# A graph layer on one core: wa for the edge weighing in two PSUM banks, TensorE's phases over three pairs of banks, and a new order of VectorE's work

## The chip, the cores and the metric

The kernel runs on one core of one Trainium2 chip. The metric is the time of one execution in microseconds (us) on the device. A core has TensorE (matmuls), VectorE, ScalarE, GpSimd and SyncE (SP); the first four compute, and SP, ScalarE and GpSimd issue DMAs here. In the rows they are PE (PEld its weight loads), DVE, ACT, POOL and SP.

## The reference

```
h = relu(layernorm(x))                                   # x 512 x 1024
feat = concat(h[src], h[dst])                            # 8704 edges
e_hh, e_oo, e_ho = relu(feat[...] @ W + b)               # 256, 1280 and 7168 edges, W 2048 x 1024 each
logit = e_f @ W_a + b_a
alpha = softmax of logit over the edges with the same dst
z = segment_sum(alpha * h[src], dst)
new = relu(concat(h, z) @ W_n + b_n)                     # W_hn for nodes 0..127, W_on for the others
out = x + new
```

All of it is float32. setup_inputs makes the edges sorted by dst.

## The kernel before, in words

**Edges of two kinds.** For the HO and OO edges, feat @ W is P[src] + Q[dst], with P and Q the products of the 512 nodes with the upper and the lower half of W (P with the bias). TensorE makes P and Q, they are stored in DRAM, and GpSimd gathers their rows for tiles of 128 edges: 56 HO tiles and 10 OO tiles. For each tile VectorE adds the two gathered rows in two halves (line 635), and weighs: relu, times wa, and a sum over 1024 columns, in one instruction (line 638), whose result is the edges' logit. GpSimd scatters the logits into tables in DRAM with a cell for each pair of nodes. The 256 HH edges (two tiles) go through a full product of their features (line 1038), half of the columns at a time, and VectorE weighs each half in its bank (line 719, weigh_hh).

**Weights.** All weights come in 40 chunks of 1 MB through four places (raw); SP issues the load of chunk c once TensorE has used chunk c - 4 (load, line 272). ScalarE and VectorE split a chunk in an upper part w_hi (line 343) and the rest w_lo (line 576), and a product is three matmuls: upper by upper, upper by rest, rest by upper (lines 909 to 911). A chunk is 4 slices (k) by 4 blocks of nodes (b) by 3 matmuls, 48 in all.

**TensorE's order**, which is written out: node_products phases 0, 1, 2 and right_products (chunks 0 to 7, HO; the halves of P, then of Q), then four phases for OO (chunks 8 to 15), among them transposes of the HH rows; then the HH edges, two halves of 16 slices, each slice followed by a group of the counting (count_group, line 1014), which counts the edges of each pair of nodes as a product of one-hot rows (VectorE, line 672) and step rows (ScalarE, line 423); then the products of h with the node weights (TOP), those that z will need (G), and the tail, where the attention is made from the tables.

**Banks.** PSUM has eight banks. Before, an even phase wrote banks 0 to 3 and an odd one banks 4 to 7, and a phase's banks were emptied while the next phase ran: by VectorE for HO's P (evacuate_p, line 620; VectorE adds the bias), by ScalarE for the others. evacuate_p(0) writes stage[:, 0], which is also the source of five DMAs that clear the pair tables, so it waits for these (s_tabs).

**VectorE's order** is a list written by hand of tiles, splits, one-hot groups and unpackings of counts. Its one-hot group g waits for TensorE's group g - 16. peak_hh (line 748) takes the maximum of the HH pair table, which SP loads behind the load of chunk 35, and that waits for TensorE's use of chunk 31. Behind peak_hh come the last tiles, g_lo (the rest part of G's products, line 741), peak_ho, and the tail.

## Time and profile before

| | us |
|---|---|
| three runs | 452.58, 463.50, 467.38 (median 463.50) |
| profiled execution | 460.47 |
| its span on the core | 458.6 |
| TensorE busy in the span | 428.7 (93%) |
| VectorE | 327.0 (71%) |
| ScalarE | 146.5 (32%) |
| GpSimd | 247.4 (54%) |

The span is from the first to the last instruction in the trace, the profiled execution's own time is 1.9 us more. Busy time is an average over stages with different limits, so it is read by stretches. A row of the timeline has the start, the duration, the engine, the line of the kernel, what is written and read, how many instructions stand behind each other, and in brackets how long the engine was idle before it and what ended that.

### The profile page before, as it was taken

To read this page: it belongs to the slowest core of one execution; us is meant where nothing else is said; L and a number is where in the kernel's file an instruction comes from. 1 tells how busy PE (TensorE), PEld (TensorE's weight loads), DVE (VectorE), ACT (ScalarE), POOL (GpSimd) and SP (SyncE) were. 2 spreads that over 40 slices of the span, in tenths; PEclk is the share of its full clock that TensorE was granted. 3 is DMA by queue.
4 is the path that set the end of the run, shared out by engine and by line. 5 is a ranking of instruction groups with operands and counts; after the bars stand their busy time and mean duration, and the time that the engine had idled before them with its cause. 6 is when DMAs were issued, how large, how long until landed. Compare 5 with 4: busy or idle time off the path is not lost.

```text
span 458.6 us, 4884 instructions
## 1 busy us (share of the span) xinstructions
PE 428.7 (93%) x1698; PEld 301.1 (66%) x1698; DVE 327.0 (71%) x614; ACT 146.5 (32%) x216; POOL 247.4 (54%) x215
## 2 busy tenths in 40 slices
PE   0999999889999999999778999999999999798996
PEld 0788888678888888864223444467778888564844
DVE  5782362023699998697735999986999289999723
ACT  3841121044131333556234850121333120603200
POOL 3030006600688887777775787877888668710000
PEclk9999999999999999999999999999999999999999
DMA  8989857995945476958657766687788998369111
GB/s 329 370 332 395 351 213 264 414 400 189 345 152 172 136 258 190 323 180 289 198 146 236 265 199 216 214 302 280 265 278 303 403 363 324 95 189 361 47 69 69
DMA packets 40456, 116.02 MB, mean 253 GB/s; under 512 B 13625, under 2 KB 13625, under 8 KB 34672
## 3 DMA queue, kind: packets, MB, share of 16 engines
q1 hardware_dynamic: 14400, 64.07, 37.4%
q0 software_dynamic: 21760, 43.26, 28.7%
q10 hardware_dynamic: 4272, 8.39, 4.8%
q8 instruction: 13, 0.21, 0.2%
q14 instruction: 11, 0.09, 0.1%
HBM read 125.93 MB, written 17.86 MB: 314 GB/s over the span
## 4 chain that ended last, share of the span: by engine, by line
PE 75%; DVE 7%; DMA 6%; issue 4%; another core or an unknown queue 3%; ACT 2%; POOL 1%; SPq 0%; POOLq 0%; DVEq 0%
PE bank L911 15%; PE bank L910 15%; PE bank L909 15%; PE bank L1038 10%; PE bank L1014 6%; DMA stage<-pairs_hh 4%; PE bank L1128 3%; PE bank L1063 3%; DVE gath L635 2%; ACT step_rows L423 2%; PE bank L1103 2%; PE bank L1117 1%; PE bank L1119 1%; PE bank L1118 1%
## 5 line engine op out<-in xcount | busy, mean ns | idle before, releaser
L909 PE MATMUL bank<-w_hi,h_t 128*128 128x512 f32 x368 | 144.6, 393 | 0.2 <-issue 0.2
L911 PE MATMUL bank<-w_hi,h_t 128*128 128x512 f32 x368 | 143.4, 390 | 1.3 <-issue 1.3
L910 PE MATMUL bank<-g_raw,h_t 128*128 128x512 f32 x368 | 143.4, 390 | 1.0 <-issue 1.0
L1202 POOL DMA_INDIRECT gath<-q_ho,q_index x56 | 70.4, 1256 | 39.9 <-DMA q_ho<-stage 23.0
L576 DVE TENSOR_TENSOR g_raw<-raw,w_hi 128x512 fp32r<-128x512 f32 x96 | 60.0, 686 | 43.5 <-ACT w_hi L343 43.4
L343 ACT ACTIVATE w_hi<-raw 128x1024 fp32r<-128x1024 f32 x48 | 48.3, 1060 | 112.3 <-PE bank L911 35.2
L635 DVE TENSOR_TENSOR gath<-gath 128x512 f32<-128x512 f32 x110 | 70.9, 685 | 17.4 <-DMA gath<-q_ho,q_index 10.7
L911 PEld LDWEIGHTS bank<-w_hi,h_t 128*128 128x128 f32 x368 | 69.2, 188 | 16.8 <-issue 2.6
L910 PEld LDWEIGHTS bank<-g_raw,h_t 128*128 128x128 f32 x368 | 69.2, 188 | 15.8 <-issue 1.6
L909 PEld LDWEIGHTS bank<-w_hi,h_t 128*128 128x128 f32 x368 | 69.3, 188 | 15.1 <-issue 0.7
L1195 POOL DMA_INDIRECT gath<-p_ho,i_src x45 | 50.6, 1125 | 50.6 <-DMA p_ho<-stage 37.2
L638 DVE SCALAR_TENSOR_TENSOR gath<-gath,wa 128x1024 f32<-128x1024 f32 x55 | 67.4, 1225 | 1.9
L1038 PE MATMUL bank<-raw,feat 128*128 128x512 f32 x128 | 63.2, 595 | 5.8 <-issue 4.6
L423 ACT ACTIVATE step_rows<-node_row,step_at 128x512 bf16<-128x512 f16 x68 | 43.8, 713 | 31.4 <-remote 22.1
L1038 PEld LDWEIGHTS bank<-raw,feat 128*128 128x128 f32 x128 | 24.0, 189 | 29.5 <-issue 25.5
L1214 POOL DMA_INDIRECT pairs_ho<-logit,cell x28 | 34.7, 1239 | 14.5 <-issue 7.0
L1214 POOL DMA_INDIRECT pairs_ho_odd<-logit,cell x28 | 33.5, 1195 | 9.9 <-issue 7.3
L1014 PE MATMUL bank<-step_rows,count_rows 128*128 128x512 bf16 x136 | 35.7, 379 | 1.4 <-issue 1.1
L1014 PEld LDWEIGHTS bank<-step_rows,count_rows 128*128 128x128 bf16 x136 | 13.0, 98 | 29.7 <-issue 21.3
L672 DVE TENSOR_SCALAR count_rows<-node_row,dst_at 128x256 bf16<-128x256 f16 x68 | 19.4, 360 | 14.5 <-remote 14.5
L1088 PE MATMUL bank<-pick 128*128 128x512 f32 x70 | 18.1, 405 | 3.3 <-DVE gath L638 3.0
L1088 PEld LDWEIGHTS bank<-pick 128*128 128x128 f32 x70 | 12.4, 188 | 8.9 <-DVE gath L638 3.1
(159 smaller groups left out, 377.5 us busy)
## 6 DMA issues: line engine op xcount, KB each, us to landing
raw<-w_chunks SPq DMA_DIRECT2D x40, 1024.0 KB
gath<-x SPq DMA_DIRECT2D x4, 512.0 KB, 5.0
h_dram<-h_sb SPq DMA_DIRECT2D x1, 2048.0 KB, 11.6
p_ho<-stage ACTq DMA_DIRECT2D x2, 1024.0 KB
p_oo<-stage ACTq DMA_DIRECT2D x2, 1024.0 KB
q_oo<-stage ACTq DMA_DIRECT2D x2, 1024.0 KB
x_place<-x SPq DMA_DIRECT2D x2, 1024.0 KB, 8.8
out<-partial SPq DMA_DIRECT2D x8, 256.0 KB, 2.0
```

Of the source, the lines that this page charges most:

```text
L423: i = nc.scalar.activation(row_src(g)[:, j], node_row[:, :], ACT.Sign, bias=step_at[:, t:t + 1])
L576: i = nc.vector.tensor_tensor(w_lo[:, c % RAW, k], raw[:, c % RAW, k], w_hi[:, upper(c), k].bitcast(f32), ALU.subtract)
L635: i = nc.vector.tensor_tensor(p[:, cols], p[:, cols], q[:, cols], ALU.add)
L638: nc.vector.scalar_tensor_tensor(out=p, in0=p, scalar=0.0, in1=wa[:, :], op0=ALU.max, op1=ALU.mult, accum_out=logit[:, at:at + 1]).then_in ...
L909: nc.tensor.matmul(to, hi, w_high, start=first, stop=False)
L910: nc.tensor.matmul(to, hi, w_low, start=False, stop=False)
L911: return nc.tensor.matmul(to, lo, w_high, start=False, stop=last)
L1014: i = nc.tensor.matmul(bank[PART_BANKS[part] + b][:, :], row_dst[:, g % HOTS, j, b * P:(b + 1) * P], row_src(g)[:, j], start=(g, j) == (fi ...
L1038: m = nc.tensor.matmul(bank[4 * half + e][:, :], feat[:, kk, e * P:(e + 1) * P], raw[:, c % RAW, k], start=False, stop=kk == 2 * KT - 1)
L1195: nc.gpsimd.indirect_dma_start(edge_p[:, slot], None, node_tab[kind][0][:, :], bass.IndirectOffsetOnAxis(ap=i_src[:, at:at + 1], axis=0)). ...
L1202: nc.gpsimd.indirect_dma_start(edge_q[:, slot], None, node_tab[kind][1][:, :], bass.IndirectOffsetOnAxis(ap=q_index[:, at:at + 1], axis=0) ...
L1214: nc.gpsimd.indirect_dma_start(pair_tab[kind][:, :], bass.IndirectOffsetOnAxis(ap=cell[:, at:at + 1], axis=0), logit[:, at:at + 1], None). ...
```

## The change

Two of the eight banks (6 and 7, now wa_places) hold wa, copied there once by ScalarE (copy_wa), and the weighing of the tiles reads wa from them. The six other banks are three pairs. A phase uses two pairs; the next one begins with the third pair, and its second pair is the one that the phase before it used first. So a chunk's matmuls run over k for blocks 0 and 1, and then over k for blocks 2 and 3, and before the second pair's first matmul stands a wait (second_pair). HH, counting, TOP and G get other banks and other waits. VectorE's order is another one.

```diff
-PART_BANKS = (2, 6, 2, 6)
+PART_BANKS = (4, 0, 2, 0)
+HH_BANKS = (2, 4)
+TOP_PAIRS = ((1, 0), (2, 1))
+G_PAIRS = ((0, 2), (1, 0))
...
+        def phase_bank(phase, b):
+            return bank[2 * ((2 * phase + b // 2) % 3) + b % 2]
...
+            def copy_wa():
+                act.wait_ge(s_const, 32)
+                act.wait_ge(s_tlo, KT)
+                for half in range(NHALF):
+                    i = nc.scalar.activation(wa_places[:, half], wa[:, half * HALF:(half + 1) * HALF], ACT.Copy)
+                i.then_inc(s_wa, 1)
...
-                nc.vector.scalar_tensor_tensor(out=p, in0=p, scalar=0.0, in1=wa[:, :], op0=ALU.max, op1=ALU.mult,
+                nc.vector.scalar_tensor_tensor(out=p, in0=p, scalar=0.0, in1=wa_places.rearrange("p a d -> p (a d)"), op0=ALU.max, op1=ALU.mult,
                                                accum_out=logit[:, at:at + 1]).then_inc(s_logit, 1)
...
+            def second_pair(phase):
+                if phase in (1, 2):
+                    pe.wait_ge(s_pev, phase + 1)
+                if phase == 4:
+                    pe.wait_ge(s_qev, Q_EVACS[1] + 2)
+                if phase in (5, 6):
+                    pe.wait_ge(s_pev, phase - 1)
+                if phase == 7:
+                    pe.wait_ge(s_qev, Q_EVACS[3])
...
             node_products(PH_HO, 1)
-            pe.wait_ge(s_pev, 2)
             node_products(PH_HO, 2)
-            pe.wait_ge(s_pev, 3)
             right_products()
...
-                if g == first and part == 1:
+                if g == first and part == 0:
                     pe.wait_ge(s_qev, Q_EVACS[4])
-                if g == first and part >= 2:
-                    pe.wait_ge(s_cev, part - 1)
+                if g == first and part == 2:
+                    pe.wait_ge(s_hhhalf, 1)
+                if g == first and part == 3:
+                    pe.wait_ge(s_cev, 2)
...
             for half in range(NHALF):
+                if half:
+                    pe.wait_ge(s_cev, 1)
                 for j in range(4):
                     c = PH_HH + 4 * half + j
...
+            g_products(0, 0, 0)
+            pe.wait_ge(s_part, 2)
+            g_products(0, 0, 1)
+            g_products(0, 1, 0)
+            g_products(0, 1, 1)
+            g_products(1, 0, 0)
+            g_products(1, 1, 0)
+            pe.wait_ge(s_glo, 1)
+            g_products(1, 0, 1)
+            g_products(1, 1, 1)
...
             unpack_part(0)
-            tiles(2)
-            one_hots(1)
+            tiles(1)
+            weigh_hh(0)
+            tiles(1)
+            one_hots(2)
+            tiles(1)
             unpack_part(1)
...
             peak_hh()
-            tiles(1)
+            tiles(2)
             split_lo(35)
-            tiles(2)
+            tiles(1)
             g_lo(0)
             tiles(1)
             peak_ho()
-            tiles(5)
+            tiles(4)
             g_lo(1)
```

In words, of VectorE's order: in both orders 32 tiles stand before one-hot group 25; before peak_hh stand 57 tiles in the old order and 58 in the new, and behind it nine and eight.

**TensorE, phase 1.** w_hi and g_raw (w_lo) are the parts of the weights, h_t is h transposed. Before, from the middle of the first chunk:

```order
L911 MATMUL bank6<-w_hi,h_t 128x512
L909 MATMUL bank7<-w_hi,h_t 128x512
L910 MATMUL bank7<-g_raw,h_t 128x512
L911 MATMUL bank7<-w_hi,h_t 128x512
L909 MATMUL bank4<-w_hi,h_t 128x512 [waits weights_lo]
L910 MATMUL bank4<-g_raw,h_t 128x512
```

Now, 24 matmuls into the phase:

```order
L946 MATMUL bank5<-w_hi,h_t 128x512
L944 MATMUL bank0<-w_hi,h_t 128x512 [waits weights_lo,p_evacuated]
L945 MATMUL bank0<-g_raw,h_t 128x512
L946 MATMUL bank0<-w_hi,h_t 128x512
L944 MATMUL bank1<-w_hi,h_t 128x512
L945 MATMUL bank1<-g_raw,h_t 128x512
```

The wait for VectorE's emptying of phase 0 (p_evacuated) stood at the first matmul of phase 2, and stands in the middle of phase 1's first chunk.

**TensorE, counting group 19**, the first of the third part, in the second half of HH. Before:

```order
L1038 MATMUL bank4<-raw,feat 128x512
L1038 MATMUL bank5<-raw,feat 128x512
L1014 MATMUL bank2<-step_rows,count_rows 128x512 [waits src_steps_ready,onehot_ready,counts_evacuated]
L1014 MATMUL bank3<-step_rows,count_rows 128x512
L1014 MATMUL bank2<-step_rows,count_rows 128x512
```

Now:

```order
L1092 MATMUL bank4<-raw,feat 128x512
L1092 MATMUL bank5<-raw,feat 128x512
L1068 MATMUL bank2<-step_rows,count_rows 128x512 [waits src_steps_ready,onehot_ready,hh_half_logits]
L1068 MATMUL bank3<-step_rows,count_rows 128x512
L1068 MATMUL bank2<-step_rows,count_rows 128x512
```

The banks are the same, but the wait is now for VectorE's weighing of the first HH half (hh_half_logits), no more for ScalarE's copy of the first part's counts.

**VectorE around the first unpacking.** count_rows are the one-hots, L683 and L712 begin an unpacking. Before, the weighing of the first HH half stood some 20 rows behind these:

```order
L672 TENSOR_SCALAR count_rows<-node_row,dst_at 128x256 [waits onehot_used]
L672 TENSOR_SCALAR count_rows<-node_row,dst_at 128x256
L683 TENSOR_TENSOR counts<-sums_buf 128x2x511 [waits counts_evacuated]
L685 ISA counts<-sums_buf 128x2 x2
L687 TENSOR_SCALAR sums_buf<-counts 128x1024 [waits vector_step]
L694 TENSOR_SCALAR counts<-counts 128x2x512 [waits vector_step]
L695 TENSOR_SCALAR counts<-sums_buf 128x2x512
L635 TENSOR_TENSOR gath<-gath 128x512 [waits vector_step,q_rows_landed1,p_rows_landed1]
```

Now, from the unpacking on:

```order
L712 TENSOR_TENSOR counts<-sums_buf 128x2x511 [waits counts_evacuated]
L714 ISA counts<-sums_buf 128x2 x2
L716 TENSOR_SCALAR sums_buf<-counts 128x1024 [waits vector_step]
L723 TENSOR_SCALAR counts<-counts 128x2x512 [waits vector_step]
L724 TENSOR_SCALAR counts<-sums_buf 128x2x512
L664 TENSOR_TENSOR gath<-gath 128x512 [waits vector_step,q_rows_landed0,p_rows_landed0]
L664 TENSOR_TENSOR gath<-gath 128x512
L667 SCALAR_TENSOR_TENSOR gath,logit<-gath,wa_places 128x1024 [waits edge_summed]
L748 SCALAR_TENSOR_TENSOR bank,logit_half<-bank,wa 128x512 [waits weights_used]
L748 SCALAR_TENSOR_TENSOR bank,logit_half<-bank,wa 128x512
```

The weighing of the HH half now comes one tile behind the unpacking.

## Rows read from the trace of the kernel before

**Rows 1.** The page's chain by engine.

```profile
PE 75%; DVE 7%; DMA 6%; issue 4%; another core or an unknown queue 3%; ACT 2%; POOL 1%; SPq 0%; POOLq 0%; DVEq 0%
```

**Rows 2.** The chain in order of time: start, us, what.

```profile
14.95 1.12 PE bank L919 x4
...
18.90 0.43 PE bank L909
...
19.75 0.23 PE bank L911
...
348.75 19.21 DMA stage<-pairs_hh
```

**Rows 3.** Timeline of VectorE around the table's maximum.

```profile
360.71 1.29 DVE L635 TENSOR_TENSOR gath<-gath 128x512 f32<-128x512 f32 x2 [4.68 <-DMA gath<-q_oo,q_index]
...
367.99 2.29 DVE L748 TENSOR_REDUCE peak<-stage 128x4 f32<-128x2048 f32 x1 [4.71 <-DMA stage<-pairs_hh]
```

**Rows 4.** Windows: us, then busy of PE, PEld, DVE, ACT, POOL; clock; DMA.

```profile
217.00:249.90 32.90, 26.25 (x68) 8.67 (x67) 17.76 (x39) 10.80 (x18) 24.89 (x23) 1.00 0.64 193
...
348.70:368.00 19.30, 19.30 (x87) 15.99 (x86) 9.80 (x17) 5.10 (x7) 13.98 (x13) 1.00 1.00 387
368.00:402.60 34.60, 31.75 (x135) 24.65 (x134) 34.15 (x51) 10.29 (x17) 25.68 (x21) 1.00 0.69 246
```

**Rows 5.** Timeline of TensorE: 96 matmuls apart; the last of G.

```profile
339.69 0.40 PE L910 MATMUL bank<-g_raw,h_t 128*128 128x512 f32 x1
...
361.46 0.39 PE L910 MATMUL bank<-g_raw,h_t 128*128 128x512 f32 x1
...
390.93 0.39 PE L911 MATMUL bank<-w_hi,h_t 128*128 128x512 f32 x1
```

**Rows 6.** Timeline of ScalarE at phase 1's start, and of VectorE's first evacuation.

```profile
41.16 2.01 ACT L343 ACTIVATE w_hi<-raw 128x1024 fp32r<-128x1024 f32 x2 [7.92 <-PE bank L911]
...
53.03 2.48 DVE L620 TENSOR_TENSOR stage<-bank,bias 128x512 f32<-128x512 f32 x4 [16.07 <-DMA pairs_hh<-stage]
```

**Rows 7.** Timeline of ScalarE: the evacuation of phase 7.

```profile
203.52 2.06 ACT L378 ACTIVATE stage<-bank 128x512 f32<-128x512 f32 x4 [5.00 <-PE bank L911]
```

**Rows 8.** Timeline of TensorE: counting groups 0, 5, 13, 18 and 19.

```profile
204.13 1.03 PE L1014 MATMUL bank<-step_rows,count_rows 128*128 128x512 bf16 x4
...
217.03 1.03 PE L1014 MATMUL bank<-step_rows,count_rows 128*128 128x512 bf16 x4
...
249.11 0.81 PE L1014 MATMUL bank<-step_rows,count_rows 128*128 128x512 bf16 x3
...
263.23 1.03 PE L1014 MATMUL bank<-step_rows,count_rows 128*128 128x512 bf16 x4
...
265.81 1.03 PE L1014 MATMUL bank<-step_rows,count_rows 128*128 128x512 bf16 x4
```

**Rows 9.** Timeline of VectorE: one-hot 25, the first unpacking, the tile behind it.

```profile
249.15 0.60 DVE L672 TENSOR_SCALAR count_rows<-node_row,dst_at 128x256 bf16<-128x256 f16 x2 [2.27 <-remote]
...
262.65 1.21 DVE L683 TENSOR_TENSOR counts<-sums_buf 128x1022 int32<-128x1022 int32 x1
...
266.28 1.29 DVE L635 TENSOR_TENSOR gath<-gath 128x512 f32<-128x512 f32 x2 [0.21 <-DVE counts L695]
```

**Rows 10.** Groups of VectorE's instructions by form: busy us, mean ns.

```profile
L635 DVE TENSOR_TENSOR gath<-gath 128x512 f32<-128x512 f32 x110 | 70.9, 685 | 17.4 <-DMA gath<-q_ho,q_index 10.7 <-DMA gath<-q_oo,q_index 4.7 <-issue 1.7
L638 DVE SCALAR_TENSOR_TENSOR gath<-gath,wa 128x1024 f32<-128x1024 f32 x55 | 67.4, 1225 | 1.9
...
L719 DVE SCALAR_TENSOR_TENSOR bank<-bank,wa 128x512 f32<-128x512 f32 x4 | 2.7, 711 | 0.0
L741 DVE TENSOR_TENSOR h_t<-bank,g_on_right 128x512 fp32r<-128x512 f32 x4 | 2.5, 680 | 0.0
```

**Rows 11.** Timeline of GpSimd: two gathers of P rows.

```profile
343.07 1.50 POOL L1195 DMA_INDIRECT gath<-p_ho,i_src  x1 [0.30 <-issue]
...
357.34 0.97 POOL L1195 DMA_INDIRECT gath<-p_oo,i_src  x1 [0.30 <-issue]
```

More of the change, by code:

```diff
@@ L401, in _ @@
             split_hi(5)
+            copy_wa()
             split_hi(6)
@@ L777, in _ @@
             dve.wait_ge(s_hd, 16)
+            dve.wait_ge(s_wa, 1)
             split_lo(9)
             split_lo(10)
-            tiles(7)
+            tiles(8)
             split_lo(11)
@@ L786, in _ @@
             tiles(3)
+            sum_h_block()
             split_lo(14)
+            tiles(3)
+            split_lo(15)
             tiles(1)
-            sum_h_block()
-            tiles(2)
-            split_lo(15)
-            tiles(2)
-            for n in range(5):
+            one_hots(1)
+            tiles(1)
+            for n in range(3):
                 one_hots(3)
                 tiles(1)
-            for n in range(2):
-                one_hots(2)
+            one_hots(2)
+            tiles(1)
+            for n in range(4):
+                one_hots(3)
                 tiles(1)
@@ L800, in _ @@
             tiles(1)
-            for n in range(3):
-                one_hots(2)
-                tiles(1)
+            one_hots(2)
+            tiles(1)
             one_hots(1)
             tiles(1)
-            for n in range(2):
-                one_hots(2)
-                tiles(1)
+            one_hots(2)
+            tiles(1)
             one_hots(1)
             unpack_part(0)
-            tiles(2)
-            one_hots(1)
+            tiles(1)
+            weigh_hh(0)
+            tiles(1)
+            one_hots(2)
+            tiles(1)
             unpack_part(1)
@@ L830, in _ @@
             split_lo(32)
-            tiles(3)
+            tiles(1)
             split_lo(33)
@@ L836, in _ @@
             peak_hh()
+            tiles(2)
+            split_lo(35)
             tiles(1)
-            split_lo(35)
-            tiles(2)
             g_lo(0)
@@ L842, in _ @@
             peak_ho()
-            tiles(5)
+            tiles(4)
             g_lo(1)
@@ L981, in transpose_rows @@
             def transpose_rows(first):
-                for k in range(first, first + KT // 2):
+                for k in range(first, first + 2):
                     for j in range(2):
@@ L1064, in _ @@
                                                  start=False, stop=kk == KT - 1)
-                        else:
-                            weights(c, k)
-                            for b in range(1, NB):
-                                if kk == 0:
-                                    add_bias(bank[4 * half + b][:, :], 3, half)
-                                m = products(bank[4 * half + b][:, :], h_t[:, 0, kk, b * P:(b + 1) * P],
-                                             h_t[:, 1, kk, b * P:(b + 1) * P], c, k, False, kk == KT - 1)
@@ new lines, in _, with g_products @@
+                    m.then_inc(s_wused, 1)
+            def g_products(q, j, pair):
+                for k in range(KC):
+                    weights(PH_G + 2 * q + j, k)
+                    kk = KC * j + k
+                    for b in (2 * pair, 2 * pair + 1):
+                        m = products(g_bank(q, b)[:, :], h_t[:, 0, kk, b * P:(b + 1) * P],
+                                     h_t[:, 1, kk, b * P:(b + 1) * P], PH_G + 2 * q + j, k, kk == 0, kk == KT - 1)
+                if pair:
+                    m.then_inc(s_wused, 1)
```

155 lines of the change are left out of this document (87 added, 68 removed).

## The prediction

> **What bounds the kernel now.** I read the page's chain first: TensorE holds 75% of the span and VectorE 7% [rows 1]. The reader is to see in it that a delay of TensorE is a delay of the end, unless something later absorbs it. In order of time it leaves TensorE for good at 348.75, with the load of the HH pair table, which lands 19.21 us later; VectorE's maximum over that table begins at 367.99, and VectorE then works on to the last tile [rows 2, 3]. The table's load stands on SP's queue behind the load of chunk 35, and that one behind TensorE's use of chunk 31. So two engines make the time in turn: TensorE until 348.7, VectorE from 368.0 to 402.6. The windows agree: TensorE is 26.25 us busy of 32.9 between 217.0 and 249.9 while VectorE is 9.80 of 19.3 us busy before the table and 34.15 of 34.6 after it [rows 4]. GpSimd, which issues the gathers and scatters, has 1% of the chain [rows 1].
>
> **The change part by part.**
>
> *The first stall, 9.0 us.* A products phase is two chunks, 96 matmuls, one each 0.227 us (339.69 to 361.46 has 96 steps) [rows 5], so 21.8 us; the first pair of banks takes 24 of them, 5.4 us. Before, phase 1 wrote banks 4 to 7 and waited for no VectorE work. Now its second pair is banks 0 and 1, which phase 0 filled and VectorE must empty. Phase 1 begins at 41.1, when chunk 1 is done and ScalarE is released [rows 6]. VectorE empties phase 0 only at 53.03, after 16.07 us of idle time for a DMA: the place it writes, stage, is the source of the five table clears [rows 6]. It ends at 55.5. Nothing in the change moves the clears, so TensorE asks at 41.1 + 5.4 = 46.5 and gets the banks at 55.5: 9.0 us idle, where before it was busy. Behind the wait stand all of TensorE's later work, the Q evacuations, the stores of Q and with them the first gathers, so VectorE's tile stream starts 9.0 us later too. Phase 1's own emptying now falls at its new end, 71.8 to 74.3, and is wanted at 77.3: no further stall. The landing of the clears is a DMA's and may move: for the range I let it come up to 3 us earlier or 2 later, 6 to 11 us, an allowance of the size of one evacuation (2.48 us) [rows 6].
>
> *The other pairs.* Phases 2 to 7 ask 5.4 us after their start for a pair that ScalarE empties in about 2.1 us after the phase before it; ScalarE begins on the signal each time (its evacuation at 203.52 took 2.06) [rows 7]. That leaves 3.3 us each: cost 0, and the cover is ScalarE standing ready. The transposes of the HH rows are the same in number, in four pieces instead of two, ScalarE's eight copies too: 0. copy_wa adds two copies of about 0.6 us on ScalarE, beside TensorE: 0.
>
> *Counting, 1.5 us.* Group 0 of the counting ran at 204.13 [rows 8]; it now writes banks 4 and 5, which the evacuation that began at 203.52 frees at 205.6 [rows 7]. Cost 1.5 us. Below it is 0 if the slow stretch that follows absorbs it.
>
> *The HH half's banks, 2.0 us.* Group 19 of the counting began at 265.81 [rows 8]. It waited for ScalarE; now it writes the banks of the first HH half and waits for VectorE's weighing of it. In VectorE's new order that weighing stands behind one-hots 25 to 30, four tiles and an unpacking. At 249.3 VectorE stands before one-hot 25 in both orders, with 32 tiles done; one group of one-hots takes 0.52, the unpacking 3.6 us (262.65 to 266.28), the weighing two instructions of 0.71 [rows 9, 10]. So 249.3 + 6 x 0.52 + 4 x 2.5 + 3.6 + 1.4 = 267.4, and up to 1 us more where one-hot 26 waits for its group. Against 265.8 that is 1.6 to 2.6 us late; I take 2.0. The ends for the range: 0 if VectorE is ahead of where it was, 4.5 if it is one tile behind.
>
> *VectorE's tile.* A tile is two adds of 0.685 us and the weighing of 1.225 us. With wa in PSUM the weighing reads one operand from there. A subtraction with one PSUM operand costs 0.680, against 0.685 with both in SBUF; the HH weighing with PSUM on both sides costs 0.711 for 512 elements, 0.026 above the add of that width [rows 10]. So between −0.005 and +0.03 us each; I take +0.01, since only an input lies in PSUM, as for the subtraction. Eight tiles on the path: 0.1 us, at most 0.2. The Trainium skill ("VectorE: DVE Perf Modes", The TRN2 errata) gives a PSUM operand 62 cycles more of fixed cost than SBUF, an estimate of 0.065 us, or 0.5 us for eight tiles; the subtraction's row here does not show it.
>
> *VectorE's order at the end, −2.5 us.* Before, nine tiles stood behind the table's maximum, now eight, the ninth having moved into idle time ahead of it (4.71 us there, and 4.68 of a row wait) [rows 3]. One tile of 2.5 us (2 x 0.685 + 1.225, overlapping a little) [rows 10] leaves the path. The split of chunk 35 now stands behind two tiles instead of one, and TensorE's new order wants it 5.4 us earlier; that and the wait for g_lo(0) cost TensorE some 2 us, which brings the end of its products from 391.3 [rows 5] to about 406, still ahead of VectorE's last tile, which ended at 402.6 and moves to about 413: 0.
>
> *Sum.* 9.0 + 1.5 + 2.0 + 0.1 − 2.5 = 10.1 us. The table's load keeps its distance to TensorE, so this reaches the end: span 458.6 + 10.1 = 468.7, and the profiled execution 460.5 + 10.1 = 470.6. The median of the three runs shown, 463.5, is 3.0 above the profiled execution; from it the sum is 473.6. I predict 472, between them. A measurement of this kernel tells about 2% from no change, 9.3 us: bounds 454.2 and 472.8.
>
> **A rule on the clock.** The granted clock reads 1.00 in each window [rows 4]; yet a matmul of the same kind took 0.43 us at 18.90 and 0.23 at 19.75: until 19.7, after the idle start, TensorE ran at half speed, 1.2 GHz, for the 4.8 us since 14.95 [rows 2]. If the 9.0 us of idle time brought that back for as long, 2.4 us more are lost: 474. The Trainium skill ("TensorE: Matmul & The Clock Gate", Part 1) says that an idle TensorE falls to 1.2 GHz and earns 2.4 GHz back by work. No row shows a fall later than the start, so it is not in the sum.
>
> **The rivals.**
>
> *GpSimd set free, and the slow stretch with it: faster.* Between 217.03 and 249.11 eight steps of HH and counting took 32.1 us, though one takes 2.58 (204.13 to 217.03 are five) [rows 8]: 11.4 us lost, with TensorE, VectorE, ScalarE each partly idle. GpSimd's DMA issues take 0.97 us where they meet no VectorE instruction, and 1.50 where they meet one: the one at 343.07 met a weighing, the one at 357.34 nothing [rows 11]. If gather pace were what holds that stretch, and the row wait of 4.68 went as well, the time would be 470.6 − 11.4 − 4.7 = 454.5, at best 452 with the HH stall gone too. The Trainium skill ("SBUF — State Buffer", Who interferes with whom) says that a VectorE instruction with two SBUF inputs holds up a GpSimd instruction that reads SBUF, and one with at most one does not; by it about a third of the 1.50s go. Against it: VectorE's idle time there is not for rows, and the row wait is followed by one for the table. It needs some 19 us of gain to pay the stall and come out faster by 9.3. Chance 0.20.
>
> *The slow stretch goes, the rest stays: no change.* Its cause is not seen in the trace; the new banks may shift it away. 470.6 − 11.4 = 459. Chance 0.15.
>
> *More coupling than I see: clearly slower.* Signals in the short deadlines come late, in phases 5 to 7 by more than the 3.3 us of slack, or the clock falls: 3 times 3 us and 2 us, 482. Chance 0.15.
>
> *The change does nothing:* wa's move may bring GpSimd nothing that anyone waits for, which the forecast assumes; the stall it can't leave out, since banks 0 and 1 are not free before VectorE has emptied them.
>
> **How the numbers follow.** Forecast 0.50: own range 466 to 478 (first stall 6 to 11, the HH half 0 to 4.5, counting 0 to 1.5, and 3 us between the two bases, not all at one end). The range that holds 8 in 10 reaches to the first rival's time and nearly to the third's: 454 to 481. Slower by over 2% takes half of the forecast and all of the coupling: 0.40. Faster is the first rival: 0.20. The rest, 0.40, is within 2%.
>
> **What would show it.** TensorE idle from about 46.5 to 55.5 with VectorE's first evacuation at 53.0; the first tile some 9 us later; the first count group behind ScalarE's copy; TensorE idle before group 19, released by VectorE's HH weighing; the table's maximum near 380; one tile fewer behind it. Wrong would be a first evacuation before 50 us, HH and counting in under 90 us, or GpSimd issues near 1.0 us together with an earlier table.

## The result, and the profile after

| | before | after |
|---|---|---|
| median, us (4 runs each) | 465.1 (452.6 to 467.4) | 477.4 (475.7 to 480.8) |
| profiled execution / its span, us | 460.5 / 458.6 | 476.1 / 474.2 |
| mean granted clock of that execution | 1.00 | 0.968 |

The ratio is 1.049 (95%: 1.033 to 1.065): **slower**. The medians differ by 12.3 us, a ratio of 1.026. The ratio and its interval, here and below, count only executions within 1.5% of their kernel's fastest, which of the four of before leaves the one of 452.6. The cost of the change is better read from the medians, and from the runs below.

The forecast had the sign and the largest cause, not the size: 472 against 477.4, or 1.8% slower than 463.5 against 4.9% by the ratio and 2.6% by the medians.

TensorE's timeline of the changed kernel at the first stall (start us, busy us, engine, line, what, and in brackets the idle time before it with its releaser):

```profile
46.13 0.39 PE L946 MATMUL bank<-w_hi,h_t 128*128 128x512 f32 x1
56.49 0.80 PE L944 MATMUL bank<-w_hi,h_t 128*128 128x512 f32 x1 [9.98 <-DVE stage L649]
57.08 0.63 PE L945 MATMUL bank<-g_raw,h_t 128*128 128x512 f32 x1
57.51 0.63 PE L946 MATMUL bank<-w_hi,h_t 128*128 128x512 f32 x1
...
60.92 0.49 PE L945 MATMUL bank<-g_raw,h_t 128*128 128x512 f32 x1
61.25 0.39 PE L946 MATMUL bank<-w_hi,h_t 128*128 128x512 f32 x1
61.48 0.40 PE L944 MATMUL bank<-w_hi,h_t 128*128 128x512 f32 x1
```

VectorE's evacuation that it waited for, which answers to [rows 6]:

```profile
53.95 2.48 DVE L649 TENSOR_TENSOR stage<-bank,bias 128x512 f32<-128x512 f32 x4 [16.99 <-DMA pairs_hh<-stage]
```

The windows over the stall and behind it (columns as in [rows 4]; the clock is the third number from the end):

```profile
47.00:57.00 10.00, 0.51 (x1) 0.50 (x2) 3.05 (x6) 0.00 (x0) 0.00 (x0) 0.69 0.59 250
57.00:62.00 5.00, 5.00 (x15) 3.88 (x14) 1.84 (x4) 0.00 (x0) 0.00 (x0) 0.59 0.56 210
```

The stall stands where it was put, 46.5 to 56.5. Behind it the matmuls are 0.43 us apart until 61, then 0.23: the engine that had idled runs at 1.2 GHz before it has 2.4 again. The eleven steps from 56.49 to 61.25 take 4.8 us where they would take 2.5: 2.3 us lost, what the prediction's part on the clock had worked out and left out of the sum. ScalarE is released by chunk 3's end at 75.4 instead of 62.9, +12.5; at the end of phase 4 (132.4 to 143.7) the delay was 11.2, so 1.2 us had been won back.

Windows of the counting stage, TensorE at its full pace and then not (columns as in [rows 4]):

```profile
217.00:233.66 16.66, 16.61 (x51) 7.29 (x51) 13.15 (x32) 7.77 (x13) 12.99 (x13) 1.00 0.74 241
233.66:252.28 18.62, 10.68 (x17) 3.16 (x16) 6.91 (x19) 5.94 (x10) 10.66 (x12) 0.63 0.63 193
```

The slow stretch of [rows 4] and [rows 8] is still there. Two groups of the counting that [rows 8] has for the kernel before, 5 and 18:

```profile
228.50 1.03 PE L1068 MATMUL bank<-step_rows,count_rows 128*128 128x512 bf16 x4
...
275.96 1.03 PE L1068 MATMUL bank<-step_rows,count_rows 128*128 128x512 bf16 x4
```

Group 5 is 11.5 us later than before. From group 7 to group 9 it took 18.6 us where two steps take 5.2 (13.5 lost; before 11.4 were lost), part of it at half clock. Group 18 is 12.7 us later, and so is group 20 behind it (281.12), so group 19 waited for nothing. The first products of the TOP stage came at 312.5 instead of 299.6, +12.9.

How late TensorE's signals came in that stretch is seen on ScalarE (three rows), with GpSimd in the two rows below. The program's step 14 needs group 2 done, which TensorE's rows end at 221.8; step 15 group 3 (224.4); step 16 group 4 (227.0):

```profile
226.28 1.33 ACT L450 ACTIVATE step_rows<-node_row,step_at 128x512 bf16<-128x512 f16 x2 [2.85 <-remote]
236.24 1.33 ACT L450 ACTIVATE step_rows<-node_row,step_at 128x512 bf16<-128x512 f16 x2 [8.63 <-remote]
247.54 7.71 ACT L450 ACTIVATE step_rows<-node_row,step_at 128x512 bf16<-128x512 f16 x12 [9.97 <-remote]
```

```profile
244.98 1.00 POOL L1271 DMA_INDIRECT gath<-q_ho,q_index  x1 [0.31 <-issue]
250.89 1.01 POOL L1283 DMA_INDIRECT pairs_ho_odd<-logit,cell  x1 [4.91 <-DVE gath L667]
```

The steps come 4.5, 12 and 20.5 us behind the groups they need. At 247.54 six steps run on end: the signals held back have come together, in the one gap that GpSimd leaves (246.0 to 250.9). VectorE's one-hots for groups 19 and 20, which wait for the same TensorE groups, start at the same two moments, 236.24 and 247.54. This coupling (**held signals** below) is in both kernels; it was not understood when the forecast was made. It isn't that TensorE waited for these late steps: what its groups 7 and 8 need, the steps and one-hots of the same numbers, had been made by 224 us. TensorE's own idle time in the stretch has no releaser in the trace, and why it slows while its signals are held is not shown.

It struck once more, where before it had not. ScalarE's split of chunk 25 needs counting group 27, done at 298.4 by TensorE's rows; it ran at 307.16 (before: 285.80, when its group had just ended), inside a gap of GpSimd from 307.1 to 313.9, and VectorE stood behind it:

```profile
307.16 2.00 ACT L362 ACTIVATE w_hi<-raw 128x1024 fp32r<-128x1024 f32 x2 [20.90 <-PE bank L1068]
...
308.25 2.50 DVE L605 TENSOR_TENSOR g_raw<-raw,w_hi 128x512 fp32r<-128x512 f32 x4 [12.54 <-ACT w_hi L362]
```

Five tiles' worth of VectorE's time went. Its later splits came late for TensorE: 0.65 us before chunk 29 and 1.01 before chunk 31, with the TOP stage's second half at 26.3 us instead of 24.1.

VectorE's timeline at the end, which answers to [rows 3]:

```profile
376.10 1.29 DVE L664 TENSOR_TENSOR gath<-gath 128x512 f32<-128x512 f32 x2 [2.72 <-DMA gath<-q_oo,q_index]
...
386.09 2.29 DVE L777 TENSOR_REDUCE peak<-stage 128x4 f32<-128x2048 f32 x1 [7.43 <-DMA stage<-pairs_hh]
...
418.26 1.88 DVE L770 TENSOR_TENSOR h_t<-bank,g_on_right 128x512 fp32r<-128x512 f32 x3
```

The table's maximum stands at 386.09, +18.1: TensorE's TOP stage ended 15.5 later, and the table took 22.7 us from there instead of 20.2. From maximum to last tile it is 32.2 us instead of 34.6: the tile taken away gave 2.4 of its 2.5. So +15.6 at the end.

TensorE's whole list of waits for VectorE (line waited for, us, times, longest), and the forms of VectorE's tile, which answer to [rows 10]:

```profile
PE bank L944 <- DVE stage L649: 10.0, 1, 10.0
PE bank L944 <- DVE g_raw L605: 5.0, 2, 4.0
...
PE bank L965 <- DVE g_raw L605: 0.6, 1, 0.6
...
PE bank L1166 <- DVE gath L906: 0.4, 1, 0.4
```

```profile
L664 DVE TENSOR_TENSOR gath<-gath 128x512 f32<-128x512 f32 x110 | 71.0, 686 | 16.6 <-DMA gath<-q_ho,q_index 12.9 <-DMA gath<-q_oo,q_index 2.7 <-DVE counts L724 0.4
L667 DVE SCALAR_TENSOR_TENSOR gath<-gath,wa_places 128x1024 f32<-128x1024 f32 x55 | 67.1, 1221 | 1.9
```

No wait for the other six pairs of banks; a weighing takes 1.221 us from PSUM, 1.225 before. The 4.0 us are for chunk 35 at 394.6, inside VectorE's last tiles, and cost nothing. GpSimd's 56 HO gathers of Q rows take 1.072 us each instead of 1.256, its scatters 0.04 longer, and VectorE's waits for HO rows did not shrink (12.9 us in all, before 10.7).

### The profile page after: what moved, and what is told of

It reads as the page before. It is cut to its first block, busy times and chain, and to the rows that moved or that the text cites. A ratio compares the mean times of both kernels' runs of the same rounds, so it can differ in the third digit from the quotient of the medians.

```text
span 474.2 us, 4892 instructions
## 1 busy us (share of the span) xinstructions
PE 431.1 (91%) x1692; PEld 305.3 (64%) x1698; DVE 326.1 (69%) x614; ACT 147.5 (31%) x218; POOL 238.0 (50%) x215
## 4 chain that ended last, share of the span: by engine, by line
PE 65%; issue 12%; POOL 9%; DMA 8%; DVE 5%; ACT 1%; SPq 0%; POOLq 0%; DVEq 0%
PE bank L944 12%; PE bank L945 12%; PE bank L946 12%; PE bank L1092 12%; PE bank L1068 6%; POOL gath L1271 3%; POOL gath L1264 3%; PE wa_places L1197 3%; DMA pairs_hh<-stage 3%; DMA pairs_ho_odd<-logit,cell 2%; PE bank L1172 1%; PE bank L1186 1%; DMA pairs_oo_odd<-logit,cell 1%; PE bank L1188 1%; PE bank L1187 1%
## 5 line engine op out<-in xcount | busy, mean ns | idle before, releaser
L944 PE MATMUL bank<-w_hi,h_t 128*128 128x512 f32 x368 | 146.5, 398 | 15.6 <-DVE stage L649 10.0
L945 PE MATMUL bank<-g_raw,h_t 128*128 128x512 f32 x368 | 145.3, 395 | 0.7 <-issue 0.7
L946 PE MATMUL bank<-w_hi,h_t 128*128 128x512 f32 x368 | 144.9, 394 | 0.0
L944 PEld LDWEIGHTS bank<-w_hi,h_t 128*128 128x128 f32 x368 | 70.3, 191 | 31.9 <-DVE stage L649 10.4
L664 DVE TENSOR_TENSOR gath<-gath 128x512 f32<-128x512 f32 x110 | 71.0, 686 | 16.6 <-DMA gath<-q_ho,q_index 12.9
L1271 POOL DMA_INDIRECT gath<-q_ho,q_index x56 | 60.0, 1072 | 40.1 <-DMA q_ho<-stage 23.3
L946 PEld LDWEIGHTS bank<-w_hi,h_t 128*128 128x128 f32 x368 | 70.3, 191 | 14.9
L667 DVE SCALAR_TENSOR_TENSOR gath<-gath,wa_places 128x1024 f32<-128x1024 f32 x55 | 67.1, 1221 | 1.9
L1283 POOL DMA_INDIRECT pairs_ho<-logit,cell x28 | 35.9, 1282 | 16.9 <-DVE gath L667 8.5
L1283 POOL DMA_INDIRECT pairs_ho_odd<-logit,cell x28 | 34.7, 1240 | 16.2 <-issue 7.9
L1092 PEld LDWEIGHTS bank<-raw,feat 128*128 128x128 f32 x128 | 25.1, 196 | 26.6 <-issue 22.4
L649 DVE TENSOR_TENSOR stage<-bank,bias 128x512 f32<-128x512 f32 x8 | 5.0, 683 | 24.3 <-DMA pairs_hh<-stage 17.0
L954 PE MATMUL bank<-ident,h_sb 128*128 128x128 f32 x24 | 5.2, 367 | 12.1 <-ACT h_sb L371 12.1
## 6 DMA issues: line engine op xcount, KB each, us to landing
h_dram<-h_sb SPq DMA_DIRECT2D x1, 2048.0 KB, 13.1
```

The source lines that it names most:

```text
L664: i = nc.vector.tensor_tensor(p[:, cols], p[:, cols], q[:, cols], ALU.add)
L667: nc.vector.scalar_tensor_tensor(out=p, in0=p, scalar=0.0, in1=wa_places.rearrange("p a d -> p (a d)"), op0=ALU.max, op1=ALU.mult, accum_o ...
L944: nc.tensor.matmul(to, hi, w_high, start=first, stop=False)
L945: nc.tensor.matmul(to, hi, w_low, start=False, stop=False)
L946: return nc.tensor.matmul(to, lo, w_high, start=False, stop=last)
L1092: m = nc.tensor.matmul(bank[HH_BANKS[half] + e][:, :], feat[:, kk, e * P:(e + 1) * P], raw[:, c % RAW, k], start=False, stop=kk == 2 * KT - 1)
```

## The experiments

The runs were measured in five sets, each on one chip and beside the kernel before. Its median there was 466.4 (e1 to e4) and 464.4 us (e5 to e8, the same chip), 449.5 (e9 to e12, a second), 450.3 (e13 to e16, a third) and 463.7 (e17, e18, a fourth). On the first and the fourth chip the kernel before ranges from 450 to 476 us, four of its ten executions beside e5 to e8 taking 452 to 455; on the other two all but one lie within 447 to 454. So times are compared within a set; where one is set against 477.4, it is against another set, and some microseconds are open. The changed kernel itself was repeated only in e13.

### The stall by itself

**e1, the stall taken away.**

```diff
-                             stage[:, 0].rearrange("p b n -> p (b n)")).then_inc(s_tabs, 16)
+                             edge_q[:, 0:2].rearrange("p a d -> p (a d)")).then_inc(s_tabs, 16)
...
-            dve.wait_ge(s_tabs, 80)
             evacuate_p(0)
...
-            nc.gpsimd.memset(stage[:, 0], EMPTY).then_inc(s_empty, 1)
+            nc.gpsimd.memset(edge_q[:, 0:2], EMPTY).then_inc(s_empty, 1)
```

> The changed kernel, with the five table clears read from the rows' buffer (edge_q, free until the first Q gathers) instead of stage, so that VectorE's first evacuation waits for chunk 1's products alone. Theory of the stall: the 10.0 us that TensorE waited at 46.5 and the half clock behind them (matmuls 0.43 us apart until 61) are nearly all of the loss. The wait goes, the granted clock stays 1.00 over 47 to 62 us, phase 4 ends near 132 instead of 143.7, and the time is 477.4 - 11 to 13 = 464 to 466, no change against the kernel before. Rival, the coupling behind it (VectorE's order, signals late in the counting stage, the later table load): the wait goes but the time stays at 470 or above. Third, the clears themselves move: the P store runs beside them and both land later, and some 2 us of the gain are lost.

Measured: 468.7 us (467.6 to 470.9), 2.3 above the kernel before, and above the 464 to 466 of the theory. VectorE's first evacuation and the clock there:

```profile
40.29 2.48 DVE L649 TENSOR_TENSOR stage<-bank,bias 128x512 f32<-128x512 f32 x4 [4.21 <-PE bank L945]
```

```profile
47.00:57.00 10.00, 10.00 (x45) 8.27 (x45) 2.50 (x4) 3.02 (x4) 0.00 (x0) 1.00 1.00 414
```

Most of the loss goes with the stall, as its theory has it: 8.7 of the 12.3 us, against the changed kernel of another set.

**e2, the stall put into the kernel before.**

```diff
+                        if base == PH_HO and n == 1 and kk == 1:
+                            pe.wait_ge(s_pev, 2)
```

> The kernel before, with one wait added: in phase 1 TensorE waits after its first 24 matmuls until VectorE has evacuated phase 0, as the changed kernel must; banks and orders stay as they were. Theory of the stall: TensorE idle for about 10 us from 46.5, half clock behind it, and 11 to 12.5 us more at the end: 476 to 478. Rival, the coupling: the kernel before has slack behind the stall, and the end moves by 5 us or less, 470 or below.

Measured: 485.6 us, but 467.3, 480.8, 490.3 and 491.7 singly. TensorE idled 10.12 us for VectorE, as in the changed kernel. The direction is the theory's; the time is above its 476 to 478, the spread is larger than the question, and the price had to wait for e12.

**e3, TensorE kept at work inside the stall.**

```diff
+                            if phase == 1:
+                                for _ in range(40):
+                                    nc.tensor.matmul(bank[6], h_t[:, 0, 0, 0:P], w_hi[:, upper(c), 0], start=True, stop=True)
                             second_pair(phase)
```

> The changed kernel, with 40 matmuls of 128x512 into a bank that nothing reads ahead of the wait in phase 1 (9.1 us of work inside the 10.0 us of waiting; they compute nothing that is used). Theory of the clock: it fell because TensorE idled; kept at work, its matmuls are 0.227 us apart right behind the wait, and 2.4 us come back there: phase 4 ends near 142.5, the time is 475 to 476. Rival: the clock falls anyway, or the 1.2 us that the phases had won back by 121 us were the slack for it: 477 to 478.

Measured: 473.8 us (471.7 to 483.6). The clock read 1.00 over 47 to 62 us. That is 3.6 less than the changed kernel of another set; see e14.

**e4, VectorE's old order in the new banks** (the lines between split_lo(9) and g_lo(1) taken from the kernel before).

> The changed kernel's banks and copy of wa, with VectorE's order of the kernel before (splits, tiles, one-hots and table maximum in the old places). By the prediction's terms the new order was worth 2.5 us at the end, and the old one leaves the HH weighing behind the last one-hots, so that counting group 19 waits some 5 us: 480 to 484. Rival: the new order's split of chunk 25 ahead of its weights (VectorE idle 12.5 us at 296 to 308) and its late split of chunk 31 (TensorE waited 4.0 us) cost more than that: 473 to 476.

Measured: 500.3 us (489.6 to 501.5), far worse than either said. TensorE before group 19:

```profile
293.57 1.49 PE L1063 MATMUL bank<-step_rows,count_rows 128*128 128x512 bf16 x3 [12.04 <-DVE bank L748]
```

The new banks need the new order: 12.0 us, not 5, when the weighing stands behind the last one-hots. That is about half of what e4 lies above the changed kernel; the rest was not taken apart. (That the 4.0 us belong to chunk 31 was misread: they are chunk 35's. The rival falls with it.)

### Held signals

**e5, the tiles' weighing with wa from SBUF** (line 667: in1=wa).

> The changed kernel, with the tiles' weighing reading wa from SBUF as before (banks, order and the copy into PSUM stay). The copy in PSUM is meant to set GpSimd free: its Q gathers' issues went from 1.256 to 1.072 us. Theory of the stall: nobody waits for GpSimd's pace, so nothing changes, 475 to 480. Rival one, wa in PSUM helps behind the stall: without it 482 or more. Rival two, a faster GpSimd does harm: in the changed kernel its issues ran without a break from 213 to 246 us, and TensorE's signals for the counting groups came 10 us apart (226.3, 236.2, 247.5) and then four within 0.3 us, while in the kernel before they came 4.3 us apart with slower issues; with wa back in SBUF the signals come closer together, VectorE's waits of 10.6 and 12.5 us shrink, and the time is 470 to 474.

Measured: 476.6 us (474.4 to 489.2), the first theory's: against the changed kernel of another set, wa in PSUM neither helps nor harms here. ScalarE's late steps stood 5.7 to 7.9 us apart instead of 10 and 11, as the second rival had it, but the time did not fall. The gathers of Q rows took 1.188 us, so only 0.12 of the 0.18 us that they had shortened are wa's place.

**e6, e7, e8, GpSimd paced by TensorE's signals.** The same edit in the changed kernel, the kernel before, and the kernel of e1:

```diff
             for n in range(LAG, T_NODE + LAG):
+                if 28 <= n <= 45:
+                    pool.wait_ge(s_oused, (n - 25) * 41 // 26 - 3)
```

> The changed kernel, with GpSimd's loop waiting at its turns 28 to 45 until TensorE's signals for the counting groups have come to within three groups (7.7 us) of where they would stand at 2.58 us a group. GpSimd then pauses exactly when the signals are late. Theory of the held signals: TensorE's signals get through when GpSimd stops issuing (in the traces each burst of them stands inside a gap of GpSimd: 249.1 in 246.0 to 250.9, 309.4 in 307.1 to 313.9); a short pause early lets them through, the slow stretch of 12 us shrinks to 5 or less, the clock stays at 1.00 there, the split of chunk 25 is on time, and the time is 477.4 - 8 to 14 = 463 to 469. Rival: TensorE is slow there for a reason of its own and GpSimd's gap is only what follows when VectorE waits; pausing GpSimd only delays rows, and the time is 477 to 485.

> The kernel before with the same waits of GpSimd. Theory of the held signals: its slow stretch (eight steps of counting in 32.1 us instead of 20.6) shrinks by 6 us or more and its end follows in part, 452 to 460, with runs closer together than 456 to 472. Rival, rows delayed and nothing gained: 466 to 475.

> The changed kernel with both edits, the table clears read from the rows' buffer (no stall in phase 1) and GpSimd paced by TensorE's signals. If stall and held signals are separate losses they add: 468.7 (the clears alone) - 8 to 14 = 455 to 461, below the kernel before. Rival, the two are one loss, the held signals only filling time that something else takes: 465 or above.

Measured: 476.1 (468.6 to 486.6), 458.9 (451.4 to 464.1) and 463.2 us (449.4 to 472.4). The window of [rows 4] in e7:

```profile
217.00:249.90 32.90, 32.80 (x103) 14.94 (x104) 24.89 (x58) 25.22 (x41) 25.68 (x24) 1.00 0.84 290
```

103 matmuls where [rows 4] has 68: the slow stretch is gone, in e6 and e8 too (102 each). e5 is their control, unpaced on the same chip: 74 matmuls in that window, and seven steps on end from 253.49, inside a gap of GpSimd from 252.6 to 258.8. In e6 ScalarE shows how (first row), beside GpSimd (second), both waiting for the same signals:

```profile
230.16 6.23 ACT L450 ACTIVATE step_rows<-node_row,step_at 128x512 bf16<-128x512 f16 x10 [5.07 <-remote]
```

```profile
230.49 0.96 POOL L1264 DMA_INDIRECT gath<-p_ho,i_src  x1 [1.54 <-remote]
```

GpSimd had stopped at 228.9; 1.2 us later five steps' signals were there. So the rival that TensorE is slow by itself falls, in this stage; e6 and e8 carry this, since e7's traced execution is a quick one (451.4) such as the kernel before has without pacing too. The end is another matter. e6 missed its 463 to 469 and stands next to its rival, e8 missed its 455 to 461. e7 met its range, 5.5 us below the kernel before by the medians, but its ratio is 1.016 (1.007 to 1.025), on the slower side: no execution of it beat the quick ones of the kernel before by more than 1 us, so no gain at the end is shown. TensorE idled 4.84 us in e6 up to 308.9 instead, and in e8 10.59 up to 304.8, both without a visible releaser, just behind the turns that were paced.

### Where signals are not held

**e9 to e12, paced to turn 60.** The edit in the kernel before (e9), the changed kernel (e10), the kernel of e1 (e11) and of e2 (e12):

```diff
+                if 28 <= n <= 48:
+                    pool.wait_ge(s_oused, min((n - 25) * 41 // 26 - 3, T_ALL // 2 - 48 + n))
+                if n in (50, 52, 53, 55, 56, 57, 60):
+                    pool.wait_ge(s_wused, {50: 26, 52: 28, 53: 29, 55: 30, 56: 31, 57: 32, 60: 33}[n])
```

> The kernel before, with GpSimd paced by TensorE's signals as in the earlier test at turns 28 to 45, and on through turn 60: to 48 by the counting groups, then at seven turns by the chunks done, each some 8 us behind their time in the trace of before. Theory of the held signals: what is left of the spread (451 to 464 with the pacing to 45) is signals held later, in the last counting groups and the products behind them; paced there too, 450 to 457, and runs closer together. Rival: the pacing to 45 took all there was, and more waits of GpSimd only delay rows: 458 to 464.

> The changed kernel with the same pacing to turn 60. With the pacing to 45 the first counting half ran at full rate, yet TensorE idled 4.8 us at 308.9 and its clock read 0.74 to 0.89 after that: the signals were held one stage later. Theory of the held signals: paced there too, the stall of 12 us (with its clock) is all that is left against the kernel before paced likewise: 462 to 468. Rival: the later idle time is VectorE's order (split of chunk 31 late), and 474 to 480 stays.

> The changed kernel with the clears read from the rows' buffer and the pacing to turn 60. Theory: the stall costs 12 us by itself, so 450 to 456, some 12 us below the changed kernel paced alike, and level with the kernel before paced alike. Rival, the new order and banks cost more than the stall: 460 or above.

> The kernel before with the wait in phase 1 (TensorE held until VectorE has evacuated phase 0) and the pacing to turn 60: the price of the stall where signals are not held. Theory of the stall: 12 us above the kernel before paced alike, 462 to 468. Rival, without held signals there is slack behind the stall: 6 us or less. Unpaced, the same wait brought 467 to 492; if the pacing brings it under 470 with a small spread, the excess there was held signals.

| kernel | us, median | ratio to before, 95% |
|---|---|---|
| before, unpaced | 449.5 | |
| e9, before | 449.6 | 0.996 (0.992 to 1.000) |
| e10, changed | 462.4 | 1.025 (1.020 to 1.030) |
| e11, changed without the stall | 449.3 | 0.997 (0.994 to 1.000) |
| e12, before with the stall | 461.5 | 1.026 (1.023 to 1.030) |

On this chip the unpaced kernel before took 447 to 453 us, so the pacing had nothing to give: e9 says nothing on held signals. The spread is small here, and the price of the stall can be read twice: 462.4 − 449.3 = 13.1 and 461.5 − 449.6 = 11.9 us. With the stall taken out, the changed kernel is level with the one before. e10 lies in its theory's range, the other three under theirs by 0.7 us at most.

### The small terms

**e13, the changed kernel again.**

> The changed kernel itself, for a second trace and for a ratio on the chip of these runs. Theory: 12 us above the kernel before wherever both run, from stall and clock alone: ratio 1.025 to 1.030. Rival: held signals cost the changed kernel more than the kernel before, since its GpSimd issues run closer together: ratio 1.035 or more on a chip where the signals are held (the kernel before at 460 or above), 1.027 where not.

Measured: 460.6 us (458.7 to 462.4) against 450.3, ratio 1.023 (1.019 to 1.028): +10.3, just under the theory's 1.025 to 1.030. The same stage as in [rows 4], unpaced:

```profile
217.00:249.90 32.90, 32.90 (x104) 14.67 (x102) 30.03 (x70) 20.30 (x32) 24.51 (x24) 1.00 0.81 269
```

No slow stretch. The stall is 9.98 us again, the matmuls behind it at half rate until 58.6 (3.1 us for seven steps of 0.23: 1.6 us lost, not 2.3). Group 19 waits, as forecast, for the weighing, and TensorE twice for a split:

```profile
262.83 1.04 PE L1068 MATMUL bank<-step_rows,count_rows 128*128 128x512 bf16 x4 [1.05 <-DVE bank L748]
...
328.32 0.80 PE L965 MATMUL bank<-bias_parts,pick 128*128 128x512 f32 x1 [3.95 <-DVE g_raw L605]
...
380.96 0.50 PE L944 MATMUL bank<-w_hi,h_t 128*128 128x512 f32 x1 [3.15 <-DVE g_raw L605]
```

**e14, TensorE at work in the stall** (e3's edit in e10).

> The changed kernel paced to turn 60, with 40 unused matmuls inside the wait of phase 1, so that TensorE does not idle there. Theory of the clock: 2.4 us of the 12 are the clock's; 459.5 to 460.5 beside 462.4 for the same kernel without them (on the chip where the kernel before takes 449.5), the matmuls behind the wait 0.227 us apart. Rival: the clock costs nothing at the end, since phases behind it had won 1.2 us back in the trace and the rest is slack: 462 to 463.

Measured: 459.1 us (453.2 to 462.6), ratio 1.014 (1.007 to 1.021). Against e13, which ran beside it without pacing, that is 1.5 us by the medians and 4 by the ratios, with intervals that overlap. The clock's share is of the size seen in the traces (1.6 to 2.3 us), and not better known than that.

**e15, wa from SBUF in e11; e16, one tile put back behind the maximum in e11.**

```diff
-            tiles(1)
             peak_hh()
-            tiles(2)
+            tiles(3)
```

> The changed kernel without the stall and paced to turn 60, with the tiles' weighing reading wa from SBUF as before. Theory: wa in PSUM brings nothing that anyone waits for, and costs nothing: 449 to 450 as with it (449.3). Rival: GpSimd's shorter issues bring rows sooner, VectorE waited some 29 us for rows in that kernel; without them 451.5 or more.

> The changed kernel without the stall and paced to turn 60, with the tile that the new order put ahead of the table's maximum moved behind it again. The prediction's term: VectorE has idle time for the table ahead of the maximum (4.4 us in this kernel's trace), so the tile behind it adds its 2.5 us to the end: 451.5 to 452.5. Rival: TensorE's products, not VectorE's tiles, end this kernel without the stall (PE is 53% of its chain), and the tile costs nothing: 449 to 450.

Measured: e15 453.2 us, ratio 1.009 (1.005 to 1.013); e16 450.0, ratio 1.000 (0.996 to 1.003). e15 stands 1.2% above e11 by the ratios, on another chip, and 3.1 us above e16, which ran beside it and differs in one tile as well. By both, wa in PSUM is worth 3 to 5 us on these chips: the rival of e15. Its trace shows little of it (the table's maximum 1.3 us later, at 361.46 instead of 360.19, Q gathers at 1.204 instead of 1.114 us). e16 against e11 is 0.3%, inside both intervals: the rival's number, but the tile's 2.5 us are neither shown nor excluded without the stall.

**e17, e18, two splits earlier** in the unpaced e1, and in e11:

```diff
+            split_lo(29)
             unpack_part(2)
             tiles(1)
-            split_lo(29)
...
             peak_hh()
+            tiles(1)
+            split_lo(35)
             tiles(2)
-            split_lo(35)
-            tiles(1)
```

> The changed kernel with the table clears read from the rows' buffer, VectorE's split of chunk 29 put ahead of the third unpacking and that of chunk 35 one tile sooner; no pacing. Theory: TensorE's waits of 4.0 us for chunk 29 and 1.5 to 3.2 for chunk 35 go, the table's load follows TensorE, and the end comes 3 to 5 us sooner: ratio 0.985 to 0.990 to the kernel before where that one takes 450. Rival: the table's landing or the rows, not TensorE, set the end by then: 0.995 to 1.0.

> The same with GpSimd paced to turn 60. Theory: level with the unpaced one where signals are not held (ratio 0.985 to 0.990), and below it by 5 us or more where they are (the kernel before at 460 or above). Rival: the pacing delays rows there, 3 us or more above the unpaced one.

Measured: 471.0 (464.2 to 476.5) and 463.3 us (457.6 to 465.8), before 463.7: neither beats it here, and the theory's ratio is missed. The wait of 3.95 us for chunk 29 is gone in both, but 6.18 us for chunk 31 stand in e18 at 345.7. The two lie 7.8 us apart by the medians, but their intervals, 1.029 (1.012 to 1.046) and 1.018 (1.006 to 1.029), overlap. The windows 300 to 335, of e17 and of e18:

```profile
300.00:335.00 35.00, 27.59 (x85) 16.36 (x84) 22.84 (x39) 4.07 (x6) 23.98 (x23) 0.90 0.66 214
```

```profile
300.00:335.00 35.00, 35.00 (x135) 25.14 (x134) 24.14 (x41) 8.67 (x12) 26.98 (x25) 1.00 0.80 287
```

What e18 gains there it had lost before. The new banks make the first counting group wait for ScalarE's evacuation of phase 7, and in e18 that wait is long:

```profile
215.21 1.48 PE L1067 MATMUL bank<-step_rows,count_rows 128*128 128x512 bf16 x3 [10.65 <-ACT stage L404]
```

TensorE's last product of phase 7 started at 201.99, ScalarE began to evacuate at 212.69, 10 us later and 1.9 us after GpSimd had stopped issuing, at 210.8, for its first paced turn. So a short deadline that the change added (priced at 1.5 us) costs 10.65 us when the signal is held. e4 and e8 have the same wait with 5.10 and 3.29 us. The two traces end 1.1 us apart (464.9 and 463.8).

No version beat the kernel before by more than its interval.

## Why the prediction was wrong

The stall, its cause and its place were right. What failed in the sum are two terms that it put at nothing: the clock behind the stall, and everything from the counting on that hangs on TensorE's late signals and VectorE's late splits. By its own steps, in the first trace of the changed kernel and in e13, where no slow stretch was seen:

| step | forecast, us | first trace | e13 |
|---|---|---|---|
| The first stall | 9.0 | 10.0 | 10.0 |
| the clock behind it | 0 (2.4 named) | 2.3, of which 1.3 was left by phase 4's end | 1.6 |
| The other pairs | 0 | 0 | 0 |
| Counting | 1.5 | 0.2 (group 5: +11.5, phase 4's end: +11.2) | not read |
| The HH half's banks | 2.0 | 0 at group 19 | 1.1 |
| VectorE's tile | +0.1 | 0 (1.221 against 1.225 us) | 0 |
| VectorE's order at the end | −2.5 | −2.5 | not read |
| splits, signals, table | 0 | 6.6 (below) | splits 3.95 and 3.15 |
| whole | 10.1 | 15.6 (sum) | 10.3 (medians; no trace of before on that chip, so the rows are not a sum) |

- **The first stall** had the right cause and place; 0.9 us came on top since the clears landed at 53.9 instead of 53.0. e1, e2, e11 and e12 show it to be the loss: with its clock it costs 11.9 to 13.1 us, and without it nothing is left.
- **The clock failed as a step of the sum.** The prediction saw a row of the start where an idle TensorE had run at half rate for 4.8 us, worked out 2.4 us, and then left them out because no row showed a later fall. The changed kernel's rows show it for 4.8 us, e13's for 3.1. In the kernel before TensorE never idles for more than 2 us behind the start, so its rows could not show what a stall of 9 us does. The rule of the Trainium skill named there ("TensorE: Matmul & The Clock Gate", Part 1) was borne out.
- **Counting and the HH half's banks** were over-priced by 1.3 and 2.0 us in this trace: ScalarE's evacuation began right on the last product of phase 7, and VectorE's weighing ended at 275.5, 3 us before group 19, not behind it. That holds where the signal is prompt; e18's 10.65 us at the same place are what it costs where it is not.
- **What was not foreseen** is the 6.6 us from the counting on: 1.4 from group 5 to TOP (the slow stretch and its half clock, less what came back behind it), 0.4 in TOP's first half, 2.2 in its second (late splits, behind VectorE's 12.5 us at chunk 25), 2.6 in the table's landing. The prediction had named the mechanism only as its third rival, signals late and the clock down, with 482 and a chance of 0.15. e6 to e8 against e5 show that the slow stretch hangs on GpSimd's unbroken issuing; that the splits' and the table's delay follow from VectorE's 12.5 us is argued from the order of the rows, and no run undid that wait alone.
- **The rival that was to make it faster**, GpSimd set free and the slow stretch with it, was wrong in its link: GpSimd's gathers of Q did get shorter (1.072 us), and the stretch stayed. What ends it is GpSimd pausing (e6, e8). That wa's place brings nothing that anyone waits for fits e5, and is 3 to 5 us off where signals are free (e15).
- **The base.** Median against median the change is +12.3, of which 10.1 were forecast: 2.2 of the 5.4 us between 472 and 477.4. Another 1.6 come from the median of before (463.5 of the three runs shown, 465.1 of four), and 1.6 from the forecast's being put below its own 473.6. The ratio of 1.049 sets the changed kernel against the one execution of 452.6. On the two chips where no slow stretch was seen both kernels are quicker (450 and 461) and the ratio is 1.023 to 1.025, so a part of the 4.9% may be held signals that this one execution escaped; it was not traced, and that is not shown.

## What to carry to other kernels

When a change makes an early phase wait for another engine, find what that engine's own wait is for: here a buffer used as the source of a DMA, cured by another source (e1, e11). Price an idle time of TensorE with the matmuls at half rate behind it, if any row of the kernel shows that after idleness. Measure two kernels side by side on one chip, and more than once: the kernel before took 449.5 us on one chip and 466 on another, and 452 to 471 within one set, more than the change costs. When a change adds a short deadline between two engines, ask how late the signal can come there, not only how long the work takes (e18).

## What the runs showed of the hardware

- TensorE's signals can reach ScalarE and VectorE 12 and 20 us after its records say it was done (steps 15 and 16 above), both engines at the same moment, and then several at once. In the counting stage of seven traces (before, after, e1 to e5) the burst stood inside a gap of GpSimd's DMA issues of 3.9 to 6.9 us; with GpSimd made to wait for the signals (e6, e7, e8) no slow stretch was left there. In the kernel before the steps came 4.3 us apart, GpSimd's own turn of three issues. What is shared there, issue, descriptors or the landing of small writes, no run separates.
- It is not in every execution, and not seen on every chip: on one of the four the changed kernel ran that stage at full rate unpaced (e13), and on another the kernel before took 449.5 us, as there, though no trace of it unpaced was taken. On the fourth e17, unpaced, ran 217 to 250 us at full rate and slowed at 300 to 335.
- TensorE kept its full clock through a 10 us wait that was filled with unused matmuls (e3, e14), and lost it for 3.1 to 4.8 us after the same wait without them.
- The weighing of 1024 elements costs the same with wa in PSUM as in SBUF (1.221 and 1.225 us), while GpSimd's gathers of Q rows shorten by 0.12 us (e5 against the changed kernel) and 0.09 us (e15 against e11).
